# Two softmax attentions with one order string for each unit in place of one for each cycle

## The reference, cut to what matters

```python
x = x + _L0_xattn_ref(_layernorm(x, axis=-1), ctx_1024, ...)
x = x + _L0_ffn_ref(_layernorm(x, axis=-1), ...)
...
q = query_states @ Wq.T + bq
k = key_value_states @ Wk.T + bk
v = key_value_states @ Wv.T + bv
...
q = q.reshape(B, SQ, NUM_HEADS, HEAD_DIM).transpose(0, 2, 1, 3) * SCALE
...
scores = jnp.einsum('bhqd,bhkd->bhqk', q, k)
attn = jax.nn.softmax(scores, axis=-1)
ctx = jnp.einsum('bhqk,bhkd->bhqd', attn, v)
ctx = ctx.transpose(0, 2, 1, 3).reshape(B, SQ, HIDDEN)
return ctx @ Wo.T + bo
```

## Time and profile before

| | us |
|---|---|
| median of 3 runs (range) | 2667.3 (2664.27 to 2671.64) |
| the profiled execution | 2666.42 |
| its span | 2664.6 |
| f=0, from its first score to its last value product | 636.8 |
| f=4, the same | 466.8 |
| f=6, the same | 647.9 |
| mean granted clock of TensorE over the span | 0.969 |

### The profile page before, as it was taken

How to read it: one execution, slowest core, us unless ns; L and a number is a source line. 1 busy time by engine, 2 the same in 40 slices (tenths; PEclk the granted TensorE clock), 3 DMA queues, 4 the chain that set the end, 5 groups by cost and what they waited for, 6 DMA issues and landing times.

```text
span 2664.6 us, 46476 instructions
## 1 busy us (share of the span) xinstructions
PE 2524.6 (95%) x18464; PEld 1257.2 (47%) x18464; DVE 1631.1 (61%) x2991; ACT 1544.1 (58%) x2621; POOL 362.5 (14%) x351
## 2 busy tenths in 40 slices
PE   7999999999899889999899999989989999999987
PEld 2434344343377668886233333268733443434433
DVE  5878788879287675442112221057587788888855
ACT  1777777777601221111787978931237777777773
POOL 3020200200003402220011010012212002010001
PEclk7999999999899999999999999999979999999998
DMA  5523334332200011002754646110043343334300
GB/s 123 75 33 43 63 42 72 37 39 26 79 26 16 1 44 28 1 1 62 103 69 68 87 54 71 48 53 1 13 62 63 42 72 42 35 63 47 42 1 32
DMA packets 68636, 125.13 MB, mean 47 GB/s; under 512 B 20979, under 2 KB 45630, under 8 KB 64966
## 3 DMA queue, kind: packets, MB, share of 16 engines
q1 hardware_dynamic: 67270, 119.73, 29.3%
q10 hardware_dynamic: 1152, 2.44, 0.4%
HBM read 41.59 MB, written 2.10 MB: 16 GB/s over the span
## 4 chain that ended last, share of the span: by engine, by line
PE 81%; DVE 9%; ACT 4%; issue 2%; SPq 2%; POOL 1%; ACTq 1%; DMA 1%; POOLq 0%; DVEq 0%
PE psum L203 38%; PE psum L749 20%; PE psum L214 13%; PE psum L2120 6%; DVE mpart L938 4%; ACT probs L816 3%; PE psum L309 1%; SPq L1063 1%; PE psum L759 0%; PE psum L2113 0%; DVE x L1408 0%; ACTq L1064 0%; DMA qst<-qp_lo 0%; PE psum L768 0%; ACTq L1063 0%
## 5 line engine op out<-in xcount | busy, mean ns | idle before, releaser
L816 ACT ACTIVATE probs<-psum 128x512 f32<-128x512 f32 (+3 forms) x2080 | 1268.1, 686 | 286.7 <-PE psum L203 278.6
L938 DVE TENSOR_REDUCE mpart<-psum 128x2 f32<-128x804 f32 x1024 | 970.9, 990 | 220.1 <-PE psum L203 206.2
L749 PE MATMUL psum<-probs,vt 128*17 128x512 f32 (+1 forms) x4992 | 650.3, 599 | 3.9 <-ACT probs L816 3.2
L203 PE MATMUL psum<-qst,kst 64*128 64x512 f32 (+3 forms) x2496 | 600.4, 438 | 19.7 <-ACT probs L816 7.8
L203 PE MATMUL psum<-kst,qst 62*128 62x402 f32 x2048 | 467.6, 412 | 26.3 <-DVE mpart L938 25.3
L203 PEld LDWEIGHTS psum<-qst,kst 64*128 64x128 f32 (+3 forms) x2496 | 282.2, 182 | 379.9 <-issue 203.5
L203 PEld LDWEIGHTS psum<-kst,qst 62*128 62x128 f32 x2048 | 225.9, 192 | 305.7 <-DVE mpart L938 194.5
L749 PEld LDWEIGHTS psum<-probs,vt 128*17 128x17 f32 (+1 forms) x4992 | 92.2, 96 | 212.9 <-issue 177.5
L214 PE MATMUL psum<-wv,ctxT 128*32 128x256 f32 (+1 forms) x2448 | 170.9, 398 | 3.3 <-ACT vt L839 3.1
L214 PE MATMUL psum<-ctxT,wk 128*32 128x512 f32 (+1 forms) x1536 | 146.4, 507 | 8.9 <-DMA ctxT<-in_ctxT 8.1
L2168 ACT ACTIVATE inner<-psum 128x512 f32<-128x512 f32 x32 | 19.2, 599 | 199.2 <-PE psum L2120 199.2
(11 more groups left out here) (339 smaller groups left out, 2609.9 us busy)
## 6 DMA issues: line engine op xcount, KB each, us to landing
kst<-kp_hi SPq DMA_DIRECT2D x144, 200.1 KB, 5.9
ctxT<-in_ctxT SPq DMA_DIRECT2D x36, 512.0 KB, 5.0
kst<-kp_lo SPq DMA_DIRECT2D x72, 200.1 KB, 5.4
qst<-qp_hi SPq DMA_DIRECT2D x144, 64.0 KB, 4.5
kst<-kp_hi SPq DMA_DIRECT2D x84, 100.1 KB, 2.9
qst<-qp_lo SPq DMA_DIRECT2D x72, 64.0 KB, 5.1
kst<-kp_lo SPq DMA_DIRECT2D x42, 100.1 KB, 3.0
stage<-in_L_ffn_W SPq DMA_DIRECT2D x16, 256.0 KB, 4.1
```

Of the source, the lines that this page charges most:

```text
L203: last = e.matmul(dst, lhsT, rhs, start=i == 0, stop=i == len(pairs) - 1)
L749: t = e.matmul(c.bank(self.acc)[32 * h:32 * h + VW, :], self.vt[0:kn, kc, self.head(g, h), :], p[0:kn, h % self.wide, :], start=kc == 0, s ...
L816: e.activation(self.probs[n % slots][0:kn, :, :], c.psum[0:kn, k:k + self.wide, :], ACT.Exp if softmax else ACT.Sigmoid, scale=DH ** -0.5) ...
L938: e.tensor_reduce(self.mpart[:, :, p * (SEQ // P) + qt, i], c.psum[:, k:k + 2, 0:MAX_WIDTH], AX.X, ALU.max).then_inc(c.drained(k), 1)
```

## The change

`cycle_steps` and `cycle_maxima` go. `unit_steps` takes one string for a whole unit, with 52 letters s, up to 32 m, 13 v and all f, and three new letters: E is `evacuate`, C `max_close` and T `max_turn`. Nothing is appended: a unit has exactly what its string names. `slot_steps` returns a None where a step does not exist in this batch, so that the letters keep their meaning. The strings hold the same steps as before for each unit (a value product or a slot step may now stand across a former cycle's border). The list of f=4 is the same, step for step, as before. In f=0 563 of 1833 steps stand at another place, in f=6 563 of 1818. One line of the table of strings is shown, of the first group of a softmax attention:

```diff
-        ("msssmvmvsssmmssmf", "msmssvssmsmvssmmf", "msmssvmsssmvssmffm", "msmssvmsssmvssmmff", "smsmsvsssvmssmffmm", "ssvmssmvssmfmssfmm", "svmsssmv"),
+        "mssmsvmssmssmsfm Esmssvssmsmvssmf msmssvsmssmvssmf fmsmssvmssmsvssm fsfmssvsmssmvssf mmCssvfmssmvssmf Tmfssmsvmsssmv",
...
-    def cycle_steps(self, u, i):
+    def unit_steps(self, u):
 
 
         f = self.f
-        taken = {"s": iter([("scores", f, u, kc, h) for kc in range(2 * i, min(2 * i + 2, len(KEY_CHUNKS)))
-                            for h in range(0, GROUP, self.wide)]),
-                 "m": iter(self.cycle_maxima(u, i)),
-                 "v": iter([("pv", f, u, kc) for kc in (2 * i - 2, 2 * i - 1)] if i else [("pv", f, u - 1, LAST_KC)] if u else []),
-                 "f": iter(self.slot_steps(u, i))}
-        steps = [step for letter in ORDERS[self.softmax][u % GROUPS][i] for step in [next(taken[letter], None)] if step]
-        steps += [step for letter in "smvf" for step in taken[letter]]
-        if i == 0 and u:
-            steps.append(("evacuate", f, u - 1))
-        if self.softmax and u + 1 < UNITS:
-            if i == 4:
-                steps.append(("max_close", f, u + 1))
-            elif i == 5:
-                steps.insert(len(steps) // 2, ("max_turn", f, u + 1))
-        return steps
...
+        chunks = range(len(KEY_CHUNKS))
+        taken = {"s": iter([("scores", f, u, kc, h) for kc in chunks for h in range(0, GROUP, self.wide)]),
+                 "m": iter(self.unit_maxima(u)),
+                 "v": iter([("pv", f, u - 1, LAST_KC) if u else None] + [("pv", f, u, kc) for kc in chunks[:-1]]),
+                 "f": iter([step for i in range(7) for step in self.slot_steps(u, i)]),
+                 "E": iter([("evacuate", f, u - 1)] if u else []),
+                 "C": iter([("max_close", f, u + 1)] if u + 1 < UNITS else []),
+                 "T": iter([("max_turn", f, u + 1)] if u + 1 < UNITS else [])}
+        return [step for letter in ORDERS[self.softmax][u % GROUPS].replace(" ", "") for step in [next(taken[letter], None)] if step]
+
+    def unit_maxima(self, u):
+
+        later = [step for v in (u + 1, u + 2) if v < UNITS for step in self.max_steps(v)]
+        return later[7:7 + len(later) // 2] if u + 2 < UNITS else later[7:]
...
-            steps = [step for i in range(7) for step in self.cycle_steps(u, i)]
+            steps = self.unit_steps(u)
```

More of the change, by code:

```diff
@@ L456, in cycle_maxima @@
-    def cycle_maxima(self, u, i):
-        if not self.softmax:
-            return []
-        ahead, first = (u + 1, 7 + 5 * i) if i < 5 else (u + 2, 5 * (i - 5))
-        return self.max_steps(ahead)[first:first + (5 if i < 6 else 2)] if ahead < UNITS else []
+        chunks = range(len(KEY_CHUNKS))
[6 more added lines that the diff above has]
+                 "T": iter([("max_turn", f, u + 1)] if u + 1 < UNITS else [])}
@@ L463, in slot_steps @@
+        return [step for letter in ORDERS[self.softmax][u % GROUPS].replace(" ", "") for step in [next(taken[letter], None)] if step]
+    def unit_maxima(self, u):
+        later = [step for v in (u + 1, u + 2) if v < UNITS for step in self.max_steps(v)]
+        return later[7:7 + len(later) // 2] if u + 2 < UNITS else later[7:]
     def slot_steps(self, u, i):
         f, (b, g) = self.f, divmod(u, GROUPS)
+        before = lambda steps: steps if b else [None] * len(steps)
+        coming = lambda steps: steps if b + 1 < BATCH else [None] * len(steps)
@@ L466, in slot_steps @@
         keys = [self.key_steps(b + 1, cc) for cc in range(KC)]
-        steps = [("turn_acc", f, u - 1)] if self.softmax and u and i == 2 else []
+        steps = [("turn_acc", f, u - 1) if u else None] if self.softmax and i == 2 else []
         if g == 0:
@@ L470, in slot_steps @@
                 steps += self.value_steps(b, 7 + i, 8 + i)
-            if self.softmax and b and i in (3, 4):
-                steps.append(("turn_ctx", f, b - 1, 2 * (i - 3)))
+            if self.softmax and i in (3, 4):
+                steps += before([("turn_ctx", f, b - 1, 2 * (i - 3))])
         elif g == 1:
-            if i < 2 and b:
-                steps += [("proj", f, b - 1, t) for t in (2 * i, 2 * i + 1)]
-            if i >= 3 and b + 1 < BATCH:
-                steps += [self.query_steps(b + 1)[0:1], self.query_steps(b + 1)[1:2], keys[0][0:1], keys[0][1:2]][i - 3]
-        elif g == 2 and i < 4 and b + 1 < BATCH:
-            steps += [keys[0][2:4], keys[1][0:1], keys[1][1:2], keys[1][2:4]][i]
-        elif g == 3 and i > 1 and b + 1 < BATCH:
-            steps += self.value_steps(b + 1, *((0, 1), (1, 3), (3, 4), (4, 6), (6, 7))[i - 2])
+            if i < 2:
+                steps += before([("proj", f, b - 1, t) for t in (2 * i, 2 * i + 1)])
+            if i >= 3:
+                steps += coming([self.query_steps(b + 1)[0:1], self.query_steps(b + 1)[1:2], keys[0][0:1], keys[0][1:2]][i - 3])
+        elif g == 2 and i < 4:
+            steps += coming([keys[0][2:4], keys[1][0:1], keys[1][1:2], keys[1][2:4]][i])
+        elif g == 3 and i > 1:
+            steps += coming(self.value_steps(b + 1, *((0, 1), (1, 3), (3, 4), (4, 6), (6, 7))[i - 2]))
         others = {(0, 5): ("ctx", f, b + 1), (2, 1): ("half", f, 4 * b + 4, 0), (2, 4): ("half", f, 4 * b + 4, 1)}
-        if (g, i) in others and b + 1 < BATCH:
-            steps.append(others[g, i])
+        if (g, i) in others:
+            steps += coming([others[g, i]])
         return steps
```

14 lines of the change are left out of this document (7 added, 7 removed).

## The result

Median 2677.4 us of 20 runs (2665.3 to 2681.9) against 2667.0 of 20 runs of the kernel before, ratio 1.0031 [1.002, 1.0041]: slower by just over what can be told from no change, 10 us above the forecast and 1.4 us outside its range. The profiled execution took 2679.1 us, its span 2677.3. Lines of the changed kernel are 6 lower than before (L932 is L938, L945 is L951, L810 is L816, L1094 is L1100).

The account below looks back on a forecast made before the run. TensorE, busy 95%, was read as setting the time, with VectorE and ScalarE bounding it locally. The terms 3.1 - 1.9 + 1.9 - 2.5 - 2.1 + 2.8 - 0.6 gave +0.7 on 2666.4: 2667 us, range 2656 to 2676.

Parts of the forecast that it names:

- Item 4: Later max_turn: its rows reach the next unit's first score late, 0.4 us for unit 1, 1.0 for unit 15: +2.8.
- Rival (b): Slower: the maxima's rows come late at units 1, 5, 9, 13 and 15 of both attentions; 2676 us, chance 0.15.
- Item 1: More stretches: 16 added in f=0 and f=6, each costing a switch of 0.19 to 0.29 us: +3.1.
- Item 2: Fewer long stretches: second group -1.9 after turn_acc and +1.9 at max_turn before the keys; third group's max_turn -2.5 us.
- rival (c): The gain comes back at the next unit's first long stretch, where ScalarE sets the time; 2669 us, inside the forecast's case.
- Item 3: First group's turns: half the waits of n_turn and turn_ctx around the last values go, -2.1 us.
- Item 5: Unit 14 loses a six-step stretch with 0.3 us of wait: -0.6 us.
- the bound: What a measurement of this kernel can tell from no change: about 0.3%, 8 us.

## Why the prediction was wrong

**Item 4, later max_turn: the step that failed.** It asked for units 1, 5, 9, 13 and 15 whether the rows come in time, and charged 1 and 15. There it was right: unit 1 waits 0.1 to 0.15 us more (said 0.4), unit 15 1.2 and 0.8 (said 1.0). The third group's units 2, 6 and 10 also got a later max_turn, and I passed over the units behind them, 3, 7 and 11. Their work between is 4.8 us (520.10 to 524.89), and I had set the rows at 4.6 "with the usual 2.71". That figure was wrong as well for this group, and with it even the right question would have found no gap, 4.6 against 4.8. It took the 0.68 us from max_turn to SP's issue from a first-group unit. In the third group ScalarE's copy stands behind exponentials and SP starts after 1.16 to 1.3 us, and the rows are there after 5.1, 5.6 once. Six gaps, 2.4 us, where the sum had 0; with the 2.0 before units 15 they are the 4.4 us of the table. Rival (b) had the mechanism and its direction, but beside unit 15 it named units 1, 5, 9, 13 as its places: 5, 9 and 13, with 5.4 us of work between, show no gap.

**The clock was no term of the sum.** I priced the attentions at 0.99 on both sides. The runs show 11 us more at half clock, about 4 us of the mean loss of 9.3 at the measured 0.37 a us (5.6 if each cost half). The means tie it to the third group's late turn (177 to 167 and 171 when it is set back or moved, 166 to 170 when it alone is added, 196 when it is later still). No single stretch could be tied to a gap: f=6's unit 3 has 0.32 us and half clock in the changed kernel, 0.32 and full clock in the one with the third group alone new, and no gap and half clock with the turn earlier. What brings such a stretch stays open. The Trainium skill (TensorE: Matmul & The Clock Gate, Part 1) says that the throttled clock is the default and activity releases it. Unit 15 of f=6 agrees in direction, with TensorE busy 83% of it at a clock of 0.83, beside 99% and 1.00 in f=0's units 1 to 13. Unit 3 is not explained by it: the clock fell behind 9.37 and 9.68 us busy of 10, and stayed full behind 9.21 in the kernel with close earlier.

**Item 1, more stretches, +3.1**: of the right size, but not isolated (16 x 0.29 is 4.6, not 4.7). The four kernels with new orders and without the third group's gaps are 2.5 to 2.9 us over the kernel before (0.37 a us), and three of them 2.0 to 2.3 in units 1 to 13 alone. They hold only six to eight of the 16 added stretches, and the number is what is left of switches, waits and savings together.

**Item 2.** turn_acc to query waits 0.22 (said 0.15). The keys' wait in the second group is 0.72 (said 0.8), the collision at L945 there as said. The waits behind the third group's max_turn are 0.55 in sum (said 0.57). What did not follow is the -2.5 for that group: without its gaps its new order gives and takes nothing (2.6 us more for 2.4 of gaps when it alone is new). That is rival (c)'s picture, a gain that comes back at the next stretch; that it went this way was not followed step by step.

**Item 3, -2.1**: not seen. Units 0 and 1, 4 and 5, 8 and 9 take 81.5, 83.7 and 83.8 us in f=0, for 81.4, 83.7 and 83.7 before; the second group's terms of item 2 lie in the same pairs. In f=6 the first two pairs even grew, by 1.2 and 0.5. In units 4 and 5 the clock is 1.00 in both kernels, so it is not that; why f=6's differ from f=0's I have not tested.

**Item 5, -0.6**: hidden, not absent. Unit 14 takes 35.6 and 37.4 us, for 35.2 and 36.2, with the gap before unit 15 in it. Without the gaps f=0's takes 34.2 for 35.0, 0.8 less at full clock; f=6's takes 35.5 for 35.0, with 3.4 us at half clock that cost some 1.3 by the 0.37.

Without the third group's rows and the clock, the sum's +0.7 would have had to be +2 to +3, still the same by the bound; the two omitted effects together carried it over. With the two savings that did not come struck out and item 4 left aside, the sum's own terms give +2.5.

## What to carry to other kernels

Where a step feeds the next unit through another engine's queue and a transfer, write down for every place it moves in how much TensorE work lies between and how long the way takes at that place, with the queue in front of it; a figure from one group does not hold for the next. Count the time at half clock over many runs beside the time itself, and take what a us of it costs from your own runs (here 0.30 to 0.37, not a half); a change of a few us can hide in it or be doubled by it, and one profile can't tell. And a wait that is taken out of an evenly loaded unit tends to come back one stretch later: 0.27 us at the keys gave nothing in the old order, 0.51 gave 0.2 to 0.3 a unit in the new one.

## What the runs showed of the hardware

From the end of SP's last issue to the first score that waits for the rows it took 1.22 to 1.27 us in most places, and 1.38 to 1.55 before unit 7 of f=0. An issue on ScalarE's queue took 0.66 us and held ScalarE idle for 0.74, as long as one on SP's. The 128x16 scaling on VectorE takes 0.17 us alone and 1.11 beside a 1.29 us subtraction on GpSimd; moved clear of it, 0.17 to 0.18 in 32 of 32 places. In f=6's unit 3, 6.8 us at the lower clock cost 2.5 us and 10.2 cost 3.7. The kernel's runs spread by their clock: of the changed kernel's 20, those at 0.970 and above took 2665 to 2671 us, those at 0.965 and below 2680 to 2682, some 2 us for each 0.001.
